# The close of a two-layer graph and expert network: the last expert product in a free bank, four additions behind the last scatter, six of the last sixteen tiles summed by TensorE and ScalarE

## What is computed

```python
x = x + _L0_gnn_ref(_layernorm(x), adj, adj, ...)     # gated graph mixing
x = x + _L0_ffn_ref(_layernorm(x), ...)               # 8 experts, one for each token
x = x + _L1_gnn_ref(_layernorm(x), adj, ...)          # two graph layers, then 4 small LSTMs
x = x + _L1_ffn_ref(_layernorm(x), router_w, w1, w2, w3)

def _L1_ffn_ref(x, router_w, w1, w2, w3):             # 8 experts, the best two for each token
    probs = softmax(flat @ router_w.T)
    topk_probs, topk_idx = top_k(probs, 2)
    ...
    h = silu(h1) * h3                                 # 341 hidden channels
    y = einsum('neh,ech->nec', h, w2)
    out = einsum('ne,nec->nc', gates, y)
```

## Time and profile before

| | us |
|---|---|
| median of 3 runs | 1085.7 |
| lowest and highest run | 1080.3, 1088.49 |
| the profiled execution | 1082.45 |
| its span in the trace | 1080.7 |
| PE busy in the span | 995.4 (92%) |

### The profile page before, as it was taken

How to read it: one execution, slowest core, us unless ns; L and a number is a source line. 1 busy time by engine, 2 the same in 40 slices (tenths; PEclk the granted TensorE clock), 3 DMA queues, 4 the chain that set the end, 5 groups by cost and what they waited for, 6 DMA issues and landing times.

```text
span 1080.7 us, 17601 instructions
## 1 busy us (share of the span) xinstructions
PE 995.4 (92%) x5432; PEld 702.9 (65%) x5433; DVE 602.6 (56%) x1832; ACT 626.1 (58%) x1156; POOL 489.6 (45%) x756
## 2 busy tenths in 40 slices
PE   5688987889998989999999999999999999999992
PEld 2333433567776844465478545644899999999992
DVE  6975797611136435655586677444747654444465
ACT  4576865434342467665433776656677776666660
POOL 5661247761371631000022005773543777777762
PEclk9799999899999999999999999999999999999996
DMA  9860001242242221000000000112121232332566
GB/s 284 343 258 1 1 15 48 70 122 86 77 126 59 77 78 64 0 1 1 0 1 1 1 1 33 53 48 68 39 61 48 74 97 74 93 95 73 198 226 199
DMA packets 79876, 86.29 MB, mean 80 GB/s; under 512 B 10114, under 2 KB 65970, under 8 KB 79026
## 3 DMA queue, kind: packets, MB, share of 16 engines
q1 hardware_dynamic: 67250, 59.28, 17.4%
q0 software_dynamic: 12544, 25.98, 7.5%
HBM read 40.64 MB, written 44.58 MB: 79 GB/s over the span
## 4 chain that ended last, share of the span: by engine, by line
PE 78%; DVE 13%; ACT 4%; issue 2%; DMA 1%; POOL 1%; ACTq 0%; DVEq 0%; SPq 0%; POOLq 0%
PE bank L1380 17%; PE bank L1407 15%; PE bank L1387 9%; PE bank L1417 8%; PE bank L1256 5%; PE bank L1131 5%; PE bank L1296 2%; PE bank L1324 2%; PE bank L1157 2%; PE bank L1097 2%; PE bank L1313 1%; PE bank L1285 1%; PE bank L1397 1%; DVE sb_R L1507 1%; PE bank L1305 1%
## 5 line engine op out<-in xcount | busy, mean ns | idle before, releaser
L1380 PE MATMUL bank<-sb_R,sb_wih_sb 128*128 128x512 f32 (+2 forms) x504 | 197.9, 543 | 1.5 <-issue 1.2
L956 ACT ACTIVATE sb_R<-bank,sb_lb_sb 128x512 f32<-128x512 f32 (+2 forms) x252 | 153.5, 634 | 72.7 <-PE bank L1387 64.0
L703 POOL DMA_INDIRECT expert_out<-sb_R,sb_slot_row x136 | 134.3, 988 | 86.6 <-ACT sb_R L979 44.9
L1380 PEld LDWEIGHTS bank<-sb_R,sb_wih_sb 128*128 128x128 f32 x504 | 95.3, 190 | 96.8 <-issue 75.7
L2193 DVE TENSOR_TENSOR sb_R<-sb_R,bank 114x384 f32<-114x384 f32 x136 | 75.3, 554 | 136.6 <-ACT sb_R L1013 90.6
L1013 ACT ACTIVATE sb_R<-bank 114x384 f32<-114x384 f32 x136 | 66.8, 491 | 101.8 <-PE bank L1407 98.1
L1417 PE MATMUL bank<-sb_BIG,sb_R 114*128 x816 | 113.9, 276 | 0.5 <-DVE sb_R L2122 0.5
L1387 PE MATMUL bank<-sb_R,sb_whh_sb 128*128 128x512 f32 (+2 forms) x288 | 111.1, 529 | 0.0
L606 POOL TENSOR_TENSOR sb_ln_p<-sb_ST 128x8 f32<-128x8 f32 (+2 forms) x14 | 3.4, 240 | 237.4 <-DVE sb_ST L1622 160.9
L678 POOL DMA_INDIRECT expert_in<-sb_R,sb_dest_i x64 | 66.4, 1037 | 84.4 <-DVE sb_dest_i L1732 63.0
L1417 PEld LDWEIGHTS bank<-sb_BIG,sb_R 114*128 114x128 f32 x816 | 101.8, 192 | 0.7 <-issue 0.7
(11 more groups left out here) (303 smaller groups left out, 1691.6 us busy)
## 6 DMA issues: line engine op xcount, KB each, us to landing
sb_XS<-expert_in SPq DMA_DIRECT2D x17, 528.0 KB, 4.0
expert_in<-sb_R SPq DMA_DIRECT2D x17, 512.0 KB, 6.4
sb_R<-expert_out SPq DMA_DIRECT2D x6, 1024.0 KB, 8.4
sorted_in<-sb_R SPq DMA_DIRECT2D x9, 512.0 KB, 5.5
sb_XS<-sorted_in SPq DMA_DIRECT2D x18, 256.0 KB, 3.1
sorted_out<-sb_R SPq DMA_DIRECT2D x18, 256.0 KB, 2.4
sb_X<-x SPq DMA_DIRECT2D x8, 512.0 KB, 7.5
out<-sb_X SPq DMA_DIRECT2D x6, 512.0 KB, 4.5
```

The costliest lines, as they stand in the source:

```text
L703: pool.indirect_dma_start(out=expert_out, out_offset=bass.IndirectOffsetOnAxis(ap=slot_row[:, i:i + 1], axis=0), in_=yd[i // 8 % RING][:, ...
L956: act.activation(gb[s][k][:, 0:c], bank[4 * s + k][:, 0:c], funcs[k], bias=lb_sb[:, (p - 1) * GATES + k:(p - 1) * GATES + k + 1]).then_inc ...
L1380: mm = pe.matmul(bank[4 * s + k][:, 0:c].rearrange("p (w b) -> p w b", b=GH), wih_sb[:, p - 1, k * P:(k + 1) * P], xin, start=True, stop=( ...
```

## The change

Three edits at the close. The down product of the last expert tile goes to `bank[0]`, and no longer waits for the gated rows of tile 133. POOL has a one-column memset behind its last indirect DMA, which raises `rows_sent`, and DVE waits for that before it adds blocks 4 and 5. The last sixteen tiles are cut into five blocks: 6 and 7 of four tiles, 8 and 9 of two, 10 of four. Blocks 9 and 10 are not added by DVE: PE sums `X` and the two expert rows in a bank, as three products with the identity (`ident`) each, and ACT copies the sum to `X`. The store of such a block waits for ACT.

```diff
+        LATEST = NH + NH // 2
+        D3_BLOCKS = [(8 * i, 8) for i in range(NF + NF // 2)]
+        D3_BLOCKS += [(LATEST, 4), (LATEST + 4, 4), (LATEST + 8, 2), (LATEST + 10, 2), (LATEST + 12, 4)]
+        D3_ON_PE = {len(D3_BLOCKS) - 2: 2, len(D3_BLOCKS) - 1: 4}
...
-                    sp.wait_ge(d3_x, 2 * i + 2)
+                    if i in D3_ON_PE:
+                        sp.wait_ge(d3_sum_out, 1 + i - min(D3_ON_PE))
+                    else:
+                        sp.wait_ge(d3_x, 2 * i + 2)
...
                 rows_home(i)
+            pool.memset(pause_p[:, :], 0.0).then_inc(rows_sent, 1)
...
+            for i, at in D3_ON_PE.items():
+                t0, n = D3_BLOCKS[i]
+                act.wait_ge(d3_sum, 1 + i - min(D3_ON_PE))
+                act.activation(X[:, t0:t0 + n, :], bank[at][:, 0:n * D].rearrange("p (n d) -> p n d", d=D),
+                               ACT.Copy).then_inc(d3_sum_out, 1)
...
-            for j in (6, 7):
-                d2_down(8 * (ND2 - 1) + j, j, er[j - 6], False)
+            d2_down(8 * ND2 - 2, 6, er[0], False)
+            d2_down(8 * ND2 - 1, 7, er[1], True, bank[0])
+
+            def d3_term(i, rows, first, last):
+                t0, n = D3_BLOCKS[i]
+                return pe.matmul(bank[D3_ON_PE[i]][:, 0:n * D].rearrange("p (n d) -> p n d", d=D), ident[:, :], rows,
+                                 start=first, stop=last)
+
+            for i, (t0, n) in enumerate(D3_BLOCKS):
+                if i in D3_ON_PE:
+                    d3_term(i, X[:, t0:t0 + n, :], True, False)
+            for i in D3_ON_PE:
+                pe.wait_ge(y_in[i], 16)
+                d3_term(i, both[i][:, :, 0, :], False, False)
+                d3_term(i, both[i][:, :, 1, :], False, True).then_inc(d3_sum, 1)
...
             for i in (8 * ND2 - 2, 8 * ND2 - 1):
                 d2_rows_out(i)
+            dve.wait_ge(rows_sent, 1)
             for i in [*D3_OF[1], *D3_OF[2]]:
-                for k in range(2):
-                    d3_add(i, k)
+                if i not in D3_ON_PE:
+                    for k in range(2):
+                        d3_add(i, k)
```

More of the change, by code:

```diff
@@ L367, in build @@
         NF = NH // 8
-        D3_BLOCKS = [(8 * i, 8) for i in range(NF + NF // 2)] + [(t, 4) for t in range(NH + NH // 2, NTILE, 4)]
+        LATEST = NH + NH // 2
+        D3_BLOCKS = [(8 * i, 8) for i in range(NF + NF // 2)]
+        D3_BLOCKS += [(LATEST, 4), (LATEST + 4, 4), (LATEST + 8, 2), (LATEST + 10, 2), (LATEST + 12, 4)]
+        D3_ON_PE = {len(D3_BLOCKS) - 2: 2, len(D3_BLOCKS) - 1: 4}
         D3_OF = (range(NF), range(NF, NF + NF // 2), range(NF + NF // 2, len(D3_BLOCKS)))
@@ L371, in build @@
         y_in = [sem(f"y_in{i}") for i in range(len(D3_BLOCKS))]
-        d3_x = sem("d3_x")
+        d3_x, d3_sum, d3_sum_out = sem("d3_x"), sem("d3_sum"), sem("d3_sum_out")
+        rows_sent = sem("rows_sent")
         out_sem = sem("out_sem")
@@ L1410, in d2_up, with d2_down @@
                 mm.then_inc(d2_h, 1)
-            def d2_down(i, j, expert, straight):
+            def d2_down(i, j, expert, straight, target=None):
+                target = target or bank[6 + j % 2]
                 pe.wait_ge(d2_m, i + 1)
@@ L1416, in d2_down @@
                 for c in range(KU):
-                    mm = pe.matmul(bank[6 + j % 2][:, 0:D], hm[j % 2][0:HC, c * P:(c + 1) * P],
+                    mm = pe.matmul(target[:, 0:D], hm[j % 2][0:HC, c * P:(c + 1) * P],
                                    down_sb[0:HC, bass.ds(expert * (KU * D) + c * D, D)],
@@ L2118, in d2_rows_out @@
                 g, j = i // 8, i % 8
+                source = bank[0] if i == 8 * ND2 - 1 else bank[6 + j % 2]
                 dve.wait_ge(d2_y, i + 1)
@@ L2121, in d2_rows_out @@
                     dve.wait_ge(d2_out[g % RING], 128 * (g // RING))
-                dve.tensor_scalar(yd[g % RING][:, j, :], bank[6 + j % 2][:, 0:D], slot_gate[:, i:i + 1], None,
+                dve.tensor_scalar(yd[g % RING][:, j, :], source[:, 0:D], slot_gate[:, i:i + 1], None,
                                   ALU.mult).then_inc(d2_yo, 1)
```

## The result

| | before | after |
|---|---|---|
| median of 8 runs | 1085.84 us | 1091.91 us |
| lowest and highest | 1079.47, 1089.18 | 1084.71, 1093.41 |
| ratio, 95% interval | | 1.0065 (1.0039 to 1.0091) |
| profiled execution, its span | 1082.45, 1080.7 us | 1088.11, 1086.2 us |

A forecast was written before the change was run, and what follows sets the result against it. The last load's landing was taken to set the end. SP's queue (+2.75) and the slower tail (+2.45), with bank and loads at nothing, made +5.2 us: 1085.7 + 5.2 = 1090.9, rounded to 1091, range 1083 to 1097.

The forecast's parts named there:

- The free bank: PE's last product in a free bank: gated rows 0.25 us earlier, covered by 2 us of POOL's work, worth nothing.
- The wait: DVE's wait before adding blocks 4 and 5: SP's last loads queue behind their stores, first load at 1070.9, +2.75 us.
- The rival that the memset runs ahead of POOL's descriptor work: At POOL's last DMA: DVE adds as early as before, only the tail costs, +2.4 us, 1088; chance 0.10.
- the additions had stalled POOL more in other executions: POOL's last turns held until the additions end in timed runs: no change, 1084 to 1087 on the median; chance 0.18.
- the row of 1.52: POOL's second-last turn, beside DVE's first addition: read as neither undisturbed (median 0.96) nor a whole addition longer.
- the 0.56 us: POOL's turn of 1.52 us against the median 0.96: excess the wait removes; if it stayed, 3.3 instead of 2.75 us.
- The loads: SP's last loads, now five pieces: bytes decide, +0; last landing kept at 8.35 us after the first issue, 1079.25.
- The sums: Six tiles on PE and ACT after the last landing: 0.86 us per 512-column instruction at the lower clock, +2.5 us.
- The term for the rise: PE's clock during the last sums: rises after 3.9 us of unbroken work, at 1081.85, minus 0.6 us.
- The slower rival: Two stores and five loads in one heap at the close: last load takes 14.5 us, +13.5, 1099; chance 0.04.
- the two forms of the rule: POOL beside DVE additions: shared SBUF port fully blocks the second; or descriptor generation needs only the write side, making the wait useless.

The follow-up runs named there:

- bank_alone: Kernel before with only the last product moved to `bank[0]`; ratio 0.9991 (0.9973 to 1.0008).
- wait_alone: Kernel before with only the memset raising `rows_sent` and DVE's wait for it before adding blocks 4 and 5; ratio 1.0038 (1.0018 to 1.0058).
- all_order: Changed kernel with SP's last loads written ahead of the stores of blocks 4 and 5; ratio 1.0020 (0.9993 to 1.0047).
- before_again: Kernel before, unchanged, profiled again on the chip of `warm_18`; 1162.68 us, span 1161.0.
- all_warm: Changed kernel with sixteen unread products on PE ahead of its wait for block 9; ratio 1.0058 (1.0035 to 1.0080).
- warm_18: Changed kernel with eighteen unread products on PE ahead of its wait for block 9; ratio 1.0027 (0.9998 to 1.0057).
- early_adds: Kernel before with the additions of blocks 4 and 5 moved in front of the last scatter; ratio 0.9981 (0.9954 to 1.0007).
- before_order: Kernel before with SP's last loads ahead of the stores of blocks 4 and 5; ratio 0.9982 (0.9958 to 1.0007).
- sum_alone: Changed kernel without the wait and the free bank, leaving the five-block cut and sums on PE and ACT; ratio 1.0026 (1.0008 to 1.0044).

## Why the prediction was right

**The direction and the size.** Predicted 1091 with 1083 to 1097, measured 1091.91. The forecast of +5.2 us for the profiled execution compares with +5.5 for its span and +6.2 for the close.

**The free bank.** Predicted nothing, covered by POOL, with the gated rows 0.25 us earlier. `bank_alone` has them 0.37 us earlier and a close 0.3 us shorter, through POOL's turn of 1.16 us, which the step did not have.

**The wait.** Predicted: rows released 1.9 us earlier, additions from 1065.15, first load 2.75 us later. By the close's own clock the additions started 3.62 us after POOL's third-last turn against 3.92 predicted, and the first load came 2.33 us later. The memset followed POOL's last turn with no gap, not 0.30 us behind it, and the load went out 0.35 us after the store (1069.42 to 1069.77), not 0.5. The chain shows why: the ten waits of the program are five steps of SP there (four of L541, one of L543), at 0.06 to 0.07 us each. The price of a step was right; their number was taken as ten. The mechanism was right: `wait_alone` shows it put in, `all_order` taken out. The rival that the memset runs ahead of POOL's descriptor work is refuted by the chain, in which DVE's wait ends with the memset behind the turn. That the additions had stalled POOL more in other executions did not show either: `before_again` has 1.52 us, as the first profile. The prediction misread the row of 1.52: the turn is longer not by a whole addition but by the rest of the one that was running (last section). So the 0.56 us did come from the additions, as the sum had it, and a turn held until all four had ended is refuted by its last turn of 0.96.

**The loads.** Predicted the last landing 8.35 us after the first issue and block 9 after 7.05; block 9 landed after 7.5 (1077.30 - 1069.77). The 0.5 us stand in SP's second issue, which took 1.07 us; in the kernel before it took 0.50. All four profiled kernels in which the loads follow the store of block 5 by 0.35 us have it (`wait_alone`, `all_warm` and `warm_18` beside the changed one), none of the others. The first load landed later after its issue too, 4.9 us instead of 4.4. So the nearness of that store, which I called a little worse and left at zero, goes with 0.5 us; by what mechanism is open.

**The sums.** Predicted 5.1 us at the lower clock, less 0.6 for a rise 3.9 us after PE resumes. Measured 5.49 with no rise: it came at 1083, after the last instruction. The term for the rise was mis-sized, by all of its 0.6 us. Block 9's four instructions were too cheap by 0.4: they took 2.1 us (ACT's copy follows at 1079.45) and not 1.7, so an instruction with 256 columns costs more than half of one with 512; block 10's took the 3.4 predicted. That PE ran at the lower level throughout and that block 10 waited for block 9's sums and not for its own load were right. `warm_18` shows what the lower level costs: 2.2 us of the close.

**The sum of it.** 0.4 us too much for the first load, 0.5 too little for the landing, 1.0 too little for PE: the mechanism was right and part of the errors cancelled. The slower rival, a heap of stores and loads that takes over 14 us, did not come: the last load of the changed kernel landed within 6.3 us of its issue.

## What to carry to other kernels

When an operation is moved back in time, look for what is queued behind those who wait for it, on the queues too: here four additions could be late for DVE at no cost, but the loads of the next batch stood in SP's queue behind their stores. A transfer that can be done before a critical one is best done before it: its bytes are carried in any case, and the last store of the program waits for them. Here `early_adds` shortened the close by 2.7 us that way, while `before_order`, which put the stores behind the loads, lengthened it by 0.8 against the same 19.7. Work given to TensorE at the end of a program, after it has been idle, must be costed at the lower clock, here 0.86 us instead of 0.45 for each of the two instructions of a 512-column float32 product. VectorE's additions were the faster ones here at either clock: a pair for four tiles takes 1.4 us, the four instructions and ScalarE's copy 2.6 at the full clock (`warm_18`).

## What the runs showed of the hardware

The moment at which PE's clock comes back after it resumes varies widely: later than 5.7 us in the changed kernel, about 3 us in `sum_alone`, and in `all_order` within the stretch from 3.7 to 4.7 us after PE began at 1143.26:

```profile
1143.00:1147.00 4.00, 3.74 (x7) 2.32 (x8) 0.59 (x2) 0.38 (x1) 0.00 (x0) 0.50 1.12 351
1147.00:1148.00 1.00, 1.00 (x3) 0.17 (x1) 0.00 (x0) 0.00 (x0) 0.00 (x0) 0.73 1.15 345
```

The same kernel took 1085.8 us on one chip and 1161.0 and 1161.1 us on two others, 7% more, while its close was the same within 0.3 us (19.5 and 19.7). Of the 80 us by which the span of `before_again` is longer, PE was busy for 29 (1024.7 and 995.4) and idle for 51. Its chain has 6% of the span in "another core or an unknown queue"; all eight profiles of the two slower chips have 5 to 7% of that, the six others none. What that stands for was not examined.

POOL's turns beside DVE's additions follow one rule. A turn that begins while an addition is running ends 0.83 us after that addition; alone it takes 0.96. From the kernel before:

```profile
1031.44 1.22 DVE L2150 TENSOR_TENSOR sb_X<-sb_R,sb_X 128x1024 f32<-128x1024 f32 x1
1032.36 1.13 POOL L703 DMA_INDIRECT expert_out<-sb_R,sb_slot_row  x1 [0.30 <-issue]
1035.84 1.22 DVE L2150 TENSOR_TENSOR sb_X<-sb_R,sb_X 128x1024 f32<-128x1024 f32 x1
1036.32 1.57 POOL L703 DMA_INDIRECT expert_out<-sb_R,sb_slot_row  x1 [0.31 <-PE bank L1407]
```

The first addition ends at 1032.66 and the turn at 1033.49, the second at 1037.06 and its turn at 1037.89. The turn of 1.52 us does the same: it begins at 1062.50, with 0.70 us of the first addition left, and ends at 1064.02. Where 0.13 us or less are left, as at 1064.33, the turn takes its 0.96 us. In all fourteen profiles, from 1000 us on (1080 us on the two slower chips), 132 turns begin during an addition, and every one agrees within 0.02 us. An addition that begins during a turn neither lengthens it nor is itself longer (1.22 us). Of the two forms of the rule that the prediction cites from the Trainium skill (SBUF — State Buffer, "Who interferes with whom"), these rows agree with the full block of POOL by an addition that came first, and not with the inference that descriptor generation is left alone. These turns also read their row numbers (`sb_slot_row`) from SBUF, and no run separates that reading from the descriptors.
